# A graph kernel's preparation reordered: degree count in one run, range check behind the scaled features, conversions on ScalarE, first bias added between the sweeps

## The reference, cut to what matters

```python
deg = segment_sum(ones, src);  dinv = where(deg > 0, rsqrt(deg), 0)
h   = x @ weight
out = segment_sum((dinv[src] * dinv[dst])[:, None] * h[src], dst) + bias
x   = layernorm(x + out)                                    # layer 0
w   = silu(ea64 @ rad_w0 + rad_b0) @ rad_w1 + rad_b1 + silu(ea32 @ sph_w0 + sph_b0) @ sph_w1 + sph_b1
q, k, v = x @ wq, x @ wk, x @ wv                            # 8 heads of 16
alpha = sum_over_head(q[dst] * w * k[src]) / sqrt(16) * edge_weight
x   = layernorm(x + segment_sum(alpha * v[src], dst) / 16)  # layer 1
```

## Time and profile before

| quantity | value |
|---|---|
| median of 3 runs | 1785.33 us (1782.15 to 1786.39) |
| profiled execution, device time | 1787.87 us |
| its span, first to last instruction | 1786.1 us |
| busy PE, DVE, ACT, POOL | 1572.9, 1384.6, 921.6, 1291.7 us |
| mean granted TensorE clock | 0.978 of full speed |
| chain that ended last, by engine | POOL 45%, issue 18%, DVE 15%, PE 11%, DMA 3% |

### The profile page before, as it was taken

How to read it: one execution, slowest core, us unless ns; L and a number is a source line. 1 busy time by engine, 2 the same in 40 slices (tenths; PEclk the granted TensorE clock), 3 DMA queues, 4 the chain that set the end, 5 groups by cost and what they waited for, 6 DMA issues and landing times.

```text
span 1786.1 us, 45640 instructions
## 1 busy us (share of the span) xinstructions
PE 1572.9 (88%) x12982; PEld 1460.7 (82%) x12982; DVE 1384.6 (78%) x3866; ACT 921.6 (52%) x1393; POOL 1291.7 (72%) x1260
## 2 busy tenths in 40 slices
PE   3359999999989986999999999999999999999995
PEld 2248888888878875998988898889989989989994
DVE  8887776777777655788778787877887787878886
ACT  0055554455555465555555555555555555555553
POOL 6757777777777715777777777777777777777771
PEclk9999999999999988999999999999999999999997
DMA  3033333333333346666666666666666666666764
GB/s 99 13 106 105 108 100 100 99 107 103 100 109 100 94 134 164 183 186 178 170 174 174 178 173 171 173 176 174 178 182 171 173 175 179 177 170 174 187 183 106
DMA packets 177667, 259.30 MB, mean 145 GB/s; under 512 B 80699, under 2 KB 91765, under 8 KB 177444
## 3 DMA queue, kind: packets, MB, share of 16 engines
q0 software_dynamic: 51840, 132.72, 27.7%
q1 hardware_dynamic: 120016, 120.99, 24.0%
q10 hardware_dynamic: 5716, 4.55, 0.8%
HBM read 235.32 MB, written 22.79 MB: 145 GB/s over the span
## 4 chain that ended last, share of the span: by engine, by line
POOL 45%; issue 18%; DVE 15%; PE 11%; DMA 3%; DVEq 3%; POOLq 1%; SPq 1%; ACT 1%; ACTq 0%
POOL arena L699 43%; PE bank L1023 4%; DVE count L1368 4%; PE bank L980 4%; DVE xsplit L1335 2%; DVE key_hot L1356 2%; DVE low_hot L1355 2%; POOL tile_f L634 1%; DMA late<-in_dst_row 1%; DVE arena L1215 1%; PE bank L990 1%; DVEq L1341 1%; DMA arena<-kv_d,idx 1%; POOLq L716 1%; DVEq L1368 1%
## 5 line engine op out<-in xcount | busy, mean ns | idle before, releaser
L699 POOL DMA_INDIRECT arena<-kv_d,idx x808 | 826.9, 1023 | 264.4 <-issue 262.6
L980 PEld LDWEIGHTS bank<-w,hid 128*128 128x128 f32 x6464 | 788.9, 195 | 21.3
L980 PE MATMUL bank<-w,hid 128*128 128x128 f32 x6464 | 797.2, 279 | 0.0
L803 ACT ACTIVATE hid<-bank,b 128x512 f32<-128x512 f32 x808 | 495.3, 682 | 314.6 <-PE bank L964 296.2
L699 POOL DMA_INDIRECT arena<-xs_d,idx x408 | 395.7, 970 | 138.5 <-issue 132.0
L962 PE MATMUL bank<-xsplit,w_hi 128*128 128x512 f32 x808 | 344.9, 438 | 80.9 <-ACT hid L803 52.2
L795 ACT ACTIVATE xsplit<-xraw 64x1024 fp32r<-64x1024 f32 x202 | 212.3, 1052 | 230.6 <-DMA xraw<-in_sph_t 212.6
L1335 DVE TENSOR_TENSOR xsplit<-xraw,xsplit 64x256 fp32r<-64x256 f32 x808 | 288.0, 414 | 7.1 <-ACT xsplit L795 0.8
L962 PEld LDWEIGHTS bank<-xsplit,w_hi 128*128 128x128 f32 x808 | 154.8, 192 | 114.6 <-ACT hid L803 60.7
L1368 DVE TENSOR_TENSOR count<-count,bank 128x200 f32 x400 | 144.8, 362 | 123.5 <-issue 58.3
L990 PE MATMUL bank<-onehot,late 128*128 128x126 f32 x1616 | 215.6, 282 | 6.2 <-DVE late L1544 4.4
(11 more groups left out here) (147 smaller groups left out, 1290.8 us busy)
## 6 DMA issues: line engine op xcount, KB each, us to landing
late<-relrow_d SPq DMA_DIRECT2D x103, 256.0 KB
xraw<-in_rad_t SPq DMA_DIRECT2D x205, 128.0 KB
xraw<-in_sph_t SPq DMA_DIRECT2D x410, 64.0 KB
w_sb<-w_d SPq DMA_DIRECT2D x52, 256.0 KB, 3.9
w_d<-w_sb SPq DMA_DIRECT2D x51, 256.0 KB
arena<-kv_d,idx POOLq DMA_INDIRECT x808
arena<-xs_d,idx POOLq DMA_INDIRECT x408
qwin<-q_d SPq DMA_DIRECT2D x101, 31.5 KB
```

The lines of the kernel that those rows point to most:

```text
L699: pool.indirect_dma_start(gath[:, k, t * width:(t + 1) * width], None, table, bass.IndirectOffsetOnAxis(ap=idx[:, pair.slot(4), j * TILES ...
L803: act.activation(hid[:, s.slot(2), c, :], hid_ps[s.sub(4, c, 4 * s.total).slot(len(hid_ps))][:, :], ACT.Silu, bias=b0[:, c:c + 1]).then_in ...
L980: mm = pe.matmul(w_ps[:, t * D:(t + 1) * D], hid[:, b, c, t * P:(t + 1) * P], w1[:, c, :], start=False, stop=(c == 3), skip_group_check=True)
```

## The change

- All 45 steps of the degree count run in one loop. The range check follows behind the scaled features, and its small matmul behind the count.
- ACT does the conversions `base_f`, `dst_f`, `tile_f`, `relrow0`, `low_f` and `hi8`, counted on the new semaphore `s_cast`. POOL keeps the subtractions and the filling of `check`.
- The split of the first-layer weights moves from POOL to DVE, behind the scaled features.
- The second-layer bias is no longer split in bf16 parts: its two rows stay float32, and PE adds them by a float32 matmul with ones.
- x is loaded straight into `nodes`, as the last but one of ACT's loads instead of the first. POOL adds the layer-0 bias chunk by chunk between the sweeps (`s_biased`).
- POOL clears `acc` at the start, ahead of `count`; the digits lie in `hid` instead of `acc`. A load of SP (`base_i`), one of the bias, and two constants go.
- DVE reads the second sweep's pass number only ahead of sweep 2. ACT runs one small Silu ahead of the passes.

```diff
 # SP
-            sp.dma_start(base_i[:, :], dst_first).then_inc(s_dst, 16)
-            sp.wait_ge(s_set, SET.b1)
-            sp.dma_start(b1_bf[0:3, :], b1_parts[0:1, :, :]).then_inc(s_b1, 16)
 # POOL
-            pool.memset(ones_bf[:, :], 1.0).then_inc(s_const, 1)
-            pool.memset(b1_bf[:, :], 0.0).then_inc(s_const, 1)
-            pool.wait_ge(s_const, 10)
+            pool.memset(acc[:, :], 0.0).then_inc(s_fill, 1)
             pool.memset(count[:, :], 0.0).then_inc(s_fill, 1)
-            step(pool.tensor_copy(base_f[:, :], base_bi[:, :]))
-            v = step(pool.tensor_copy(dst_f[:, :], dst_ei[:, :]))
-            step_wait(v)
+            pool.wait_ge(s_cast, CAST.dst)
...
-            v = step(pool.tensor_copy(tile_f[:, :], tile_i[:, :]))
+            pool.wait_ge(s_cast, CAST.tile)
...
-            step(pool.tensor_copy(relrow0[:, :, :], dst_rowi[:, :, :]))
-            step(pool.tensor_copy(low_f[:, :], half_i[:, 0, :]))
-            v = step(pool.tensor_scalar(hi8[:, :], half_i[:, 1, :], float(NARROW), None, ALU.mult))
...
-            v = step(pool.tensor_tensor(nodes[:, :, :], x_raw, b_l0_sb[:, :].unsqueeze(1).to_broadcast([P, NB, D]),
-                                        ALU.add))
-            pool.wait_ge(s_hot, DEG_STEPS)
-            pool.memset(acc[:, :], 0.0).then_inc(s_fill, 1)
...
+            for c in range(CHUNKS):
+                own = nodes[:, blocks(c)[0]:blocks(c)[-1] + 1, :]
+                pool.tensor_tensor(own, own, b_l0_sb[:, :].unsqueeze(1).to_broadcast([P, len(blocks(c)), D]),
+                                   ALU.add).then_inc(s_biased, 1)
             pool.wait_ge(s_conv, CHUNKS)
 # ACT
-            act.dma_start(x_raw, x_pad).then_inc(s_wts, 16)
...
+            act.dma_start(nodes[:, :, :], x_pad).then_inc(s_wts, 16)
             act.dma_start(cut[:, :], cut_e).then_inc(s_wts, 16)
+            act.wait_ge(s_dst, 32)
+            act.activation(base_f[:, :], base_bi[:, :], ACT.Copy).then_inc(s_cast, 1)
+            act.activation(dst_f[:, :], dst_ei[:, :], ACT.Copy).then_inc(s_cast, 1)
+            act.wait_ge(s_tile, 32)
+            act.activation(tile_f[:, :], tile_i[:, :], ACT.Copy).then_inc(s_cast, 1)
+            act.activation(relrow0[:, :, :], dst_rowi[:, :, :], ACT.Copy).then_inc(s_cast, 1)
...
-            act.wait_ge(s_set, SET.all)
+            act.activation(low_f[:, :], half_i[:, 0, :], ACT.Copy).then_inc(s_cast, 1)
+            act.activation(hi8[:, :], half_i[:, 1, :], ACT.Copy, scale=float(NARROW)).then_inc(s_cast, 1)
+            act.activation(table[:, :], b0[:, 0:1], ACT.Silu).then_inc(s_table, 1)
             act.wait_ge(s_pre, PRE.passes)
 # PE
-            run_steps(pe, DEG_LOOP, count_src)
-            pe.wait_ge(s_const, 10)
+            run_steps(pe, DEG_STEPS, count_src)
+            pe.wait_ge(s_wts, WEIGHTS)
+            pe.wait_ge(s_const, 8)
+            pe.matmul(bank[4][:, :], ones[0:2, :], b1_wide, start=True, stop=True).then_inc(s_bias, 1)
             pe.wait_ge(s_pre, PRE.viol)
             pe.matmul(bank[0][:, 0:1], ones[:, :], small[:, 2:3], start=True, stop=True).then_inc(s_viol, 1)
-            for c in range(DEG_LOOP, DEG_STEPS):
-                count_src(Step(c, total=DEG_STEPS))
...
-                        pe.matmul(w_ps[:, :], ones_bf[:, :], b1_bf[:, :], start=True, stop=False, skip_group_check=True)
+                        pe.matmul(w_ps[:, :], ones[0:2, :], b1_wide, start=True, stop=False, skip_group_check=True)
 # DVE: digits, 45 steps in one run, the two halves of half_i, degrees, dinv, scaled features, then
+            dve.wait_ge(s_whi, 1)
+            v = pre(dve.tensor_tensor(w0_lo[:, :, :], w0_raw[:, :, :], w0_hi[:, :, :].bitcast(F32), ALU.subtract))
+            pre_wait(v)
+            for j in (1, 3):
+                own = slice(j * SPH, (j + 1) * SPH)
+                v = pre(dve.tensor_tensor(w0_hi[own, 1, :], w0_raw[own, 1, :], w0_hi[own, 1, :].bitcast(F32), ALU.subtract))
+            dve.wait_ge(s_set, SET.rel)
...
+            dve.wait_ge(s_viol, 1)
...
+            dve.wait_ge(s_set, SET.all)
+            dve.wait_ge(s_cast, CAST.all)
...
-            n_pass1, n_pass2 = passes(dve, 1), passes(dve, 2)
+            n_pass1 = passes(dve, 1)
...
                 if b % CHUNK == 0:
+                    dve.wait_ge(s_biased, b // CHUNK + 1)
                     dve.wait_ge(s_conv, b // CHUNK + 1)
...
+            n_pass2 = passes(dve, 2)
             dve.wait_ge(s_clear, 1)
```

More of the change, by code:

```diff
@@ L286, in build @@
         lo_hot = lo_hot.rearrange("p (k t a) -> p k t a", k=4, t=DEG_COLS)
-        dig, to = part_bf(acc, 0, 4 * DEG_STEPS * DEG_COLS)
+        digits = hid[:, :, :, :].rearrange("p a b c -> p (a b c)")
+        dig, to = part_bf(digits, 0, 4 * DEG_STEPS * DEG_COLS)
         dig = dig.rearrange("p (j c k) -> p j c k", j=2, k=2)
@@ L646, in _ @@
                                     ALU.subtract))
[L647 to L651, removed]
+            v = step(pool.tensor_tensor(coff[:, rest:DENSE], tile_f[:, rest:DENSE],
+                                        tile_f[:, rest:rest + 1].to_broadcast([P, DENSE - rest]), ALU.subtract))
             assert 2 + whole == SPANS
@@ L658, in _ @@
             assert v == SET.rel, v
-            step(pool.tensor_copy(relrow0[:, :, :], dst_rowi[:, :, :]))
-            pool.wait_ge(s_pre, PRE.half)
-            step(pool.tensor_copy(low_f[:, :], half_i[:, 0, :]))
-            v = step(pool.tensor_scalar(hi8[:, :], half_i[:, 1, :], float(NARROW), None, ALU.mult))
[L663 to L683, removed]
-            v = step(pool.tensor_tensor(nodes[:, :, :], x_raw, b_l0_sb[:, :].unsqueeze(1).to_broadcast([P, NB, D]),
-                                        ALU.add))
+            step(pool.tensor_copy(span_f[0:1, 0:1], tile_f[0:1, 0:1]))
+            step(pool.tensor_copy(span_f[0:1, 1:1 + whole], spans(tile_f)[0:1, :, 0]))
+            v = step(pool.tensor_copy(span_f[0:1, 1 + whole:2 + whole], tile_f[0:1, rest:rest + 1]))
             assert v == SET.all, v
-            pool.wait_ge(s_hot, DEG_STEPS)
-            pool.memset(acc[:, :], 0.0).then_inc(s_fill, 1)
             pool.wait_ge(s_pre, PRE.passes)
@@ L920, in _ @@
         def _(pe):
+            b1_wide = b1_rows[:, :].unsqueeze(1).to_broadcast([2, TILES, D])
             def count_src(s):
@@ L1199, in _ @@
             v = pre(dve.tensor_scalar(dig_i[:, 1, :], src_i[:, :], DIGITS.bit_length() - 1, None, ALU.logical_shift_right))
-            pre(dve.tensor_scalar(half_i[:, 0, :], src_i[:, COLS1:COLS], LO - 1, None, ALU.bitwise_and))
-            v_half = pre(dve.tensor_scalar(half_i[:, 1, :], src_i[:, COLS1:COLS], LO.bit_length() - 1, None, ALU.logical_shift_right))
-            assert v_half == PRE.half, v_half
             pre_wait(v)
@@ L1217, in hots @@
                 last.then_inc(s_hot, 1)
-            run_steps(dve, DEG_LOOP, hots)
-            dve.wait_ge(s_set, SET.rel)
-            pre(dve.tensor_reduce(small[:, 0:1], check, AX.X, ALU.max))
-            v = pre(dve.tensor_reduce(small[:, 1:2], check, AX.X, ALU.min))
-            pre_wait(v)
-            v = pre(dve.tensor_scalar(small[:, 0:1], small[:, 0:1], WIN - 0.5, None, ALU.is_gt))
-            pre_wait(v)
-            v = pre(dve.scalar_tensor_tensor(out=small[:, 2:3], in0=small[:, 1:2], scalar=-0.1, in1=small[:, 0:1],
-                                             op0=ALU.is_lt, op1=ALU.add))
-            assert v == PRE.viol, v
-            for c in range(DEG_LOOP, DEG_LOOP + 4):
-                hots(Step(c, total=DEG_STEPS))
-            dve.wait_ge(s_viol, 1)
-            v = pre(dve.tensor_scalar(small[:, 3:4], bank[0][:, 0:1], 0.5, None, ALU.is_lt))
-            pre_wait(v)
-            pre(dve.tensor_scalar(passes_i[:, 0:1], small[0:1, 3:4], float(1 - WINDOWS1), float(WINDOWS1),
-                                  ALU.mult, ALU.add))
-            v = pre(dve.tensor_scalar(passes_i[:, 1:2], small[0:1, 3:4], float(1 - WINDOWS2), float(WINDOWS2),
-                                      ALU.mult, ALU.add))
-            assert v == PRE.passes, v
-            for c in range(DEG_LOOP + 4, DEG_STEPS):
-                hots(Step(c, total=DEG_STEPS))
+            run_steps(dve, DEG_STEPS, hots)
+            pre(dve.tensor_scalar(half_i[:, 0, :], src_i[:, COLS1:COLS], LO - 1, None, ALU.bitwise_and))
+            v = pre(dve.tensor_scalar(half_i[:, 1, :], src_i[:, COLS1:COLS], LO.bit_length() - 1, None, ALU.logical_shift_right))
+            assert v == PRE.half, v
             dve.wait_ge(s_degmm, DEG_STEPS)
@@ L1269, in _ @@
                 assert v == PRE.xs + j, v
-            dve.wait_ge(s_set, SET.prep)
+            dve.wait_ge(s_whi, 1)
[4 more added lines that the diff above has]
+                v = pre(dve.tensor_tensor(w0_hi[own, 1, :], w0_raw[own, 1, :], w0_hi[own, 1, :].bitcast(F32), ALU.subtract))
+            assert v == PRE.w0, v
+            dve.wait_ge(s_set, SET.rel)
+            pre(dve.tensor_reduce(small[:, 0:1], check, AX.X, ALU.max))
```

(42 more changed lines are left out.)

35 lines of the change are left out of this document (14 added, 21 removed).

## The result

The changed kernel took 1772.96 us (median of 5 runs, 1772.45 to 1777.6), the kernel before 1782.23 us beside it (1781.86 to 1786.39). The ratio is 0.9943, 95% interval 0.9924 to 0.9963. A second group of executions gave 0.9934 (0.9914 to 0.9955). So the change is worth 9 to 12 us, where 7.9 was forecast. Between the two profiled executions, 1787.87 and 1772.56 us, lie 15.3 us; not all of that belongs to the change, as the milestones show. One execution each of the changed kernel in the second group (2953.63 us) and of e5 (3562.89 us) ran far slower than the rest; both count in the medians given and in no ratio.

A forecast was written before the change was run, and what follows sets the result against it. Preparation was taken as a chain mainly through DVE, sweep 1 as PE and POOL running level. 18.7 - 1.4 - 0.8 - 1.8 - 4 = 10.7, less 0.2 and 2.6, gives 7.9 us off: 1777.4 us, range 1771 to 1783.

The forecast's parts named there:

- cheap ports: Rival: POOL's readers slip in free and the additions fit in gaps; gain 16.5 us, or 12 us (1773); chance 0.15.
- (a): Preparation, DVE: the wait for POOL to fill `check` goes, 6.5 us saved.
- (b): Degree count, DVE: eight instructions slowed by POOL return to 0.605 us each, 10.3 us saved.
- (c): End of preparation, DVE: the second register load moves to the start of sweep 2, 0.9 us saved.
- (g): Start of the count: it comes later, as POOL clears `acc` ahead of `count`, 1.8 us lost.
- (d): Preparation, DVE: the `tensor_scalar` held by the clearing of `acc` is freed, 0.95 us saved.
- (e): Preparation: the split of w0 moves onto DVE, 1.4 us added.
- (f): Preparation: the check's round trip through PE, hidden under the count before, now open, 0.8 us added.
- (h): POOL's reading instructions beside the count: 4 us lost, between 6 if let in and 2.4 if kept out.
- (i): Between the sweeps: POOL's bias addition makes DVE wait, 2.6 us lost, bounds 0 and 5.
- Late first loads: Rival: first loads take 7.5 us, first matmul at 101.5; 2.4 us less gain, 1779.8 us; chance 0.08.
- slower gathers: Rival: sweep 1's gathers slow to a mean of 1003 ns, 1791 us and above; chance 0.05.

The follow-up runs named there:

- e5: Kernel before with only the count in one run and the check behind the scaled features, POOL's list unchanged: 2505.64 us on another chip, ratio 1.0002.
- e6: Kernel before with only x loaded into `nodes` and POOL adding the layer-0 bias between the sweeps: 2504.37 us on another chip, ratio 0.998.
- e4: Kernel before with only the conversions `base_f`, `dst_f`, `tile_f`, `relrow0` moved to ACT: 2510.98 us on another chip, ratio 1.001.
- e3: Changed kernel with the count's loop cut in two, DVE waiting between for `rel`: 1765.44 us, ratio to before 0.9887; again 1774.59 us, 0.9926.
- e2: Changed kernel with POOL's clearing of `acc` and `count` behind the count's first step: 1765.75 us, ratio to before 0.9888.
- e7: e2 with the load of x moved back to the head of ACT's loads: 1772.41 us, ratio to before 0.9909.

## Why the prediction was right, point by point

The direction, the place and most of the terms held: the time fell by 9.3 us where 7.9 was forecast, inside its range. The preparation shrank by more than summed, 14.5 us at the first matmul instead of 10.7; at 95.33 that matmul lies outside the 96 to 103 that I had named as a sign. That the two totals agree better than this is partly luck: at the first gather of sweep 2 the kernel is 12.1 us ahead, where my terms give 8.1, and single executions scatter by 5 us. The 1772.96 us is the number of the cheap ports, whose mechanism did not occur.

(a), (b) The wait for `check` and the eight slowed instructions went as priced: 0.45 us of waiting is left, and the count runs at 0.604 us an instruction throughout. e6 shows that the bias addition alone is 6.6 us of (b). e5 shows that the order alone brings 4.8 us and e4 that the conversions bring 1.5; the three sum to 12.9 of 14.5, which is no decomposition, because each part was taken alone, and the 14.5 also hold (c), (g) and the split on DVE.

(c) 2.6 us from the last preparing instruction to L1314 have become 1.0, so 1.6 us and not 0.9. But the second register load is the smaller part of it. e5 keeps both loads, and there the same stretch takes 1.62 us; so leaving out one is worth 0.6. The other 1.0 is that the loads got shorter. DVE's first load took 1.20 us and its second 0.65; in e5 they take 0.55 and 0.31, and in the changed kernel the one that is left takes 0.55:

```profile
87.31 0.55 DVEq L416
```

Before, as in e4 and e6, ACT's own two loads ran in the same stretch and were as slow (0.94 and 1.13 us, against 0.29 and 0.48 after). What slowed them was not tested.

(d) The `tensor_scalar` is held after all, by POOL's `near` instead of by clearing: 0.94 us, a gain of 0.2 and not 0.95.

(e) The split takes 2.1 us instead of 1.4, some 0.5 of it held: in e3, where POOL is done by then, it takes 1.6. (f) The round trip: 0.7 us for 0.8.

(g) The size was right, 1.6 us for 1.8, and the mechanism partly wrong. I had DVE slip in between the two clearings; it was held through both. e2 confirms that the clearing was the cause: without it beside the digits the count starts 7.4 us earlier.

(h) This is the term that was mis-sized. I took 4 us as a middle between POOL's readers interleaving and being kept out. They were kept out, `rel` for 51.54 us. I had priced that case at 2.4. It came to about 0.7: 0.45 us of waiting and 2.3 us in which DVE's instructions behind the count are held (8.19 us from the first copy of the degrees to the end of the split, 5.92 in e3), less the 2.0 that `rel` no longer takes from the count. Of the 2.3 us, 0.8 stand in (d) and 0.5 in (e) already; without them (h) is a gain of 0.5. With that the terms sum to 6.5 + 10.3 + 1.6 + 0.2 - 2.1 - 0.7 - 1.6 + 0.5 = 14.7 us, against 14.5 measured. I had put the filling of `check` at 80.5, with 3 us of waiting for DVE; it was done at 78.6, and DVE came at 78.2, 2.1 us later than I had it. The case by the Trainium skill's rule, 6 us, did not occur, and the row of `tile_f` was the better guide.

First gather: forecast 92.5, measured 87.68. The numbers of passes came at 83.6 instead of 86.9, for the reasons above, and the index transfer of 85.21 was there within 2.5 us, where I had allowed 4.

(i) 1.0 us, not 2.6, by the steadier stretch over ten profiles, and 1.7 on the other chip; the pieces of 1.27 us ran far ahead of DVE's rows, and one instruction was held for long.

The gain on its way: 14.5 us at the first matmul, 13.5 at the end of sweep 1, 12.1 at the first gather of sweep 2. Up to there the parts are accounted for, but for 1 us in sweep 1. The rest of the profiled difference lies in sweep 2, which took 1071.9 us from first to last gather before, 1068.3 after, and 1067.9 to 1075.7 in eight profiles of the changed kernel and its variants. That is scatter, and it is the larger part of what makes single executions of one kernel differ by 5 us and more. The rivals: the cheap ports came nearest, with POOL costing almost nothing, though because it was shut out and not because it slipped in. Late first loads and slower gathers did not occur (967 ns a gather against 970).

## What to carry to other kernels

When a stretch of two-input DVE instructions runs without a gap, look at what POOL has to read in it: a reading instruction that arrives in the midst may stand until the stretch ends, even if it is as short as `tile_f`, a conversion of 400 columns. Writers (clearing) belong beside such a stretch, and not beside DVE's `tensor_scalar`. An instruction moved away from one engine's list should be checked for what stands in its place: in e4 the next one was held even longer. Compare milestones of profiles when totals scatter by 5 us; a first matmul repeats to 0.1 us.

## What was not expected of the hardware

Whether POOL is shut out or takes turns depends, in all rows here, on what stands ahead of the instruction. Asked for in the running count after a pause of POOL, a reading instruction stood for 25.9, 36.3, 39.4, 44.8 and 51.5 us in five kernels; in the last of them 82 instructions of the count started meanwhile. Asked for right behind a clearing it stood for 46.1 us (e7). Asked for right behind another reading instruction of POOL that was being served, it was served after one DVE instruction at most, ten times in a row in e3; and before, `rel` behind the conversion of `dst_f` took its 1.97 us though the count had started at 13.25. How the two engines settle this was not tested further.

And on one chip the kernel before takes 2507 us instead of 1785. TensorE's granted clock is 0.83 to 0.88 there from the first sweep on, after a preparation at full clock, in all four profiles taken there. The clock does not account for all of it: in e4 the most frequent matmul (L981) took 301 ns against 279 before, 8% more, where the whole kernel took 40% more. What else is slower on that chip stays open.
